# Expert stage of a small language-model tower: wide count matmuls, ups of two chunks in turn, row norm on ScalarE, top two by match and replace

## What is computed

```
h = h + attention(layernorm(h))
x = layernorm(h)                                  # rows of 128
probs, idx = top_k(softmax(x @ router_w.T), 2)    # 64 experts, two chosen
pos = place of each (token, expert) among the tokens of that expert, in order
keep = pos < 128                                  # capacity of an expert
y = gelu(x @ w1.T + b1) @ w2.T + b2               # one shared feed-forward net, 128 -> 512 -> 128
out = h + y * sum over the chosen and kept experts of their probs
```

## Time and profile before

| what | value |
|---|---|
| median of 3 runs | 1189.69 us (1189.53 to 1195.04) |
| the profiled execution's own time | 1188.89 us |
| its span, first to last instruction | 1187.0 us |
| TensorE busy | 1024.0 us (86%) |
| VectorE busy | 953.1 us (80%) |
| ScalarE busy | 756.7 us (64%) |
| GpSimd busy | 211.2 us (18%) |
| mean granted TensorE clock | 0.923 of full |

### The profile page before, as it was taken

The page is one execution under the profiler, slowest core; times in us unless marked ns, Lnnn a source line. Parts: engine busy times, 40 slices in busy tenths (PEclk is TensorE's granted clock), DMA queues, the critical chain, the costliest instruction groups (busy, mean ns, idle before and its releaser), DMA issues. The chain is left out here.

```text
span 1187.0 us, 30085 instructions
## 1 busy us (share of the span) xinstructions
PE 1024.0 (86%) x12144; PEld 545.5 (46%) x12144; DVE 953.1 (80%) x1872; ACT 756.7 (64%) x1446; POOL 211.2 (18%) x317
## 2 busy tenths in 40 slices
PE   0585777559999999999999999999999849887988
PEld 0474665403444344344443443444444225746666
DVE  3576866788998898998988988888898257979784
ACT  1557658404887878878877877787878825142332
POOL 7666845320000000000000000000000010202020
PEclk9987677857999999999999999999999987989979
DMA  3222956360332423424333342432300241314011
GB/s 76 63 77 89 200 112 209 118 133 3 56 75 38 80 51 58 72 41 71 57 60 51 58 73 38 75 56 38 73 11 12 81 150 36 93 53 124 0 35 37
DMA packets 81334, 84.06 MB, mean 71 GB/s; under 512 B 23985, under 2 KB 58358, under 8 KB 81206
## 3 DMA queue, kind: packets, MB, share of 16 engines
q1 hardware_dynamic: 70710, 73.87, 28.5%
q0 software_dynamic: 2048, 4.20, 1.5%
q10 hardware_dynamic: 8448, 4.20, 1.2%
HBM read 47.73 MB, written 34.08 MB: 69 GB/s over the span
## 5 line engine op out<-in xcount | busy, mean ns | idle before, releaser
L1114 DVE TENSOR_REDUCE b_neg_max<-psM 128x1 f32<-128x1024 f32 x512 | 603.3, 1220 | 70.1 <-PE psM L1012 66.7
L1086 ACT ACTIVATE prob<-psS 128x512 f32<-128x512 f32 x1024 | 529.1, 604 | 161.3 <-PE psS L1032 161.3
L1012 PE MATMUL psM<-ks,qs 96*32 96x512 bf16 x4096 | 418.3, 394 | 18.2 <-PEq L875 14.5
L1032 PE MATMUL psS<-qs,ks 99*32 99x512 bf16 x4096 | 407.6, 382 | 9.1 <-ACT prob L1086 4.5
L1046 PE MATMUL psO<-prob,vs 128*17 128x512 f32 x2048 | 267.2, 592 | 0.2 <-ACT prob L1086 0.2
L1032 PEld LDWEIGHTS psS<-qs,ks 99*32 99x32 bf16 x4096 | 116.0, 96 | 209.7 <-ACT prob L1086 106.9
L1012 PEld LDWEIGHTS psM<-ks,qs 96*32 96x32 bf16 x4096 | 115.6, 98 | 174.9 <-DVE b_neg_max L1114 85.9
L907 POOL CAST mpart<-b_neg_max 128x16 bf16<-128x16 f32 x32 | 6.3, 196 | 636.8 <-DVE b_neg_max L1114 624.8
L1046 PEld LDWEIGHTS psO<-prob,vs 128*17 128x17 f32 x2048 | 61.1, 99 | 50.5 <-ACT prob L1086 1.1
L329 POOL DMA_INDIRECT emb<-in_table,idx x64 | 63.3, 989 | 19.6 <-issue 14.6
L1310 ACT ACTIVATE y_t<-c_psT 128x512 f32<-128x512 f32 x16 | 9.6, 597 | 87.3 <-PE c_psT L1370 87.3
(11 more groups left out here) (134 smaller groups left out, 1058.2 us busy)
## 6 DMA issues: line engine op xcount, KB each, us to landing
qk_parts<-qk_part SPq DMA_DIRECT2D x48, 256.0 KB, 2.8
qs<-qk_parts SPq DMA_DIRECT2D x192, 64.0 KB, 3.6
ks<-qk_parts SPq DMA_DIRECT2D x96, 128.0 KB, 4.2
o_cols<-ot SPq DMA_DIRECT2D x32, 256.0 KB, 4.2
qs<-mpart_t SPq DMA_DIRECT2D x384, 1.0 KB, 1.7
v_rows<-vrow SPq DMA_DIRECT2D x16, 272.0 KB, 2.9
vs<-v_rows SPq DMA_DIRECT2D x8, 544.0 KB, 6.2
h_rows<-h SPq DMA_DIRECT2D x16, 256.0 KB, 4.9
```

What stands on the lines that cost most here:

```text
L1012: last = nc.tensor.matmul(psM[count % MRING][q * HP:(q + 1) * HP, n, :], qs[buf][0:DATA_ROWS, half, hh, at + q * HP:at + (q + 1) * HP], ks ...
L1032: last = nc.tensor.matmul(psS[unit % SRING][q * HP:(q + 1) * HP, :], ks[buf][0:ROWS, GH * gb + hh, tile * P + q * HP:tile * P + (q + 1) * HP],
L1086: nc.scalar.activation(prob[step % PRING][:, hh, :], psS[unit % SRING][:, :], ACT.Exp).then_inc(score_free, 1)
L1114: nc.vector.tensor_reduce(neg_max[e % 2][:, unit:unit + 1], psM[count % MRING][:, :, :], AX.XY, ALU.max, negate=True).then_inc(max_free, 1)
```

## The change

`count_chosen` writes the counts of all four tiles of a chunk with one matmul of 256 columns (triangle) and three of 192, 128 and 64 columns (ones), and the totals with four as before: 8 instead of 14. `up` and `gelu` go through the pieces in another order: of chunks 0 and 1 the first two pieces each, then the last two each, then chunks 2 and 3 likewise. The row norm moves from VectorE to ScalarE, as an activation with a scale and an offset for each row; GpSimd makes the offset from the negated mean, which VectorE gives it. In ScalarE's order all 16 norms of a round stand between `tanh` and `copy_y_t`; in VectorE's order `result` of chunks 2 and 3 follows `statistics`. The probabilities stay undivided by their sum, and the gate is multiplied by the inverse of the sum. `choose` finds the eight largest, overwrites all but the first two by -2, replaces the matching probabilities by -1, and marks what is below zero. The loops on the engines are written out in all five programs, so waits and addresses are constants, and `wait_apart` is used no more here. Shortened:

```diff
--- before.py
+++ after.py
...
+        PIECES = [(pair + w, k + j) for pair in range(0, WAYS, SLOTS) for k in range(0, FK, 2) for w in range(SLOTS) for j in range(2)]
+
+        def grown(r, w, k):
+
+            return r * WAYS * FK + PIECES.index((w, k)) + 1
...
-            for t in range(TILES):
-                dst = psR[w][:, 1, t * EXPERTS:(t + 1) * EXPERTS]
-                for u in range(t):
-                    nc.tensor.matmul(dst, c["ones"][:, :], chosen[w][:, u, :], start=u == 0, stop=False)
-                nc.tensor.matmul(dst, c["later"][:, :], chosen[w][:, t, :], start=t == 0, stop=True)
+            marks = chosen[w][:, :, :].rearrange("p t e -> p (t e)")
+            nc.tensor.matmul(psR[w][:, 1, :], c["later"][:, :], marks, start=True, stop=False)
+            for t in range(1, TILES):
+                nc.tensor.matmul(psR[w][:, 1, t * EXPERTS:], c["ones"][:, :], marks[:, 0:(TILES - t) * EXPERTS],
+                                 start=False, stop=t == TILES - 1)
...
                 def root(r):
                     for w in range(WAYS):
                         pool.wait_ge(eps_done, r * WAYS + w + 1)
-                        nc.gpsimd.tensor_tensor(rstd[w][:, :], var_eps[w][:, :], c["neg_half"][:, 0:TILES], ALU.pow).then_inc(rstd_done, 1)
+                        nc.gpsimd.tensor_tensor(rstd[w][:, :], var_eps[w][:, :], c["neg_half"][:, 0:TILES], ALU.pow).then_inc(root_done, 1)
+                        pool.wait_ge(root_done, r * WAYS + w + 1)
+                        nc.gpsimd.tensor_tensor(offset[w][:, :], neg_mean[w][:, :], rstd[w][:, :], ALU.mult).then_inc(rstd_done, 1)
...
-                        wait_apart(pool, h2_done, r * WAYS + w + 1 + WAYS)
+                        pool.wait_ge(h2_done, r * WAYS + w + 1 + WAYS)
...
+                def norm(r):
+                    for w in range(WAYS):
+                        act.wait_ge(rstd_done, r * WAYS + w + 1)
+                        for t in range(TILES):
+                            last = nc.scalar.activation(y[w][:, t, :], h2[w][:, t, :], ACT.Identity,
+                                                        bias=offset[w][:, t:t + 1], scale=rstd[w][:, t:t + 1])
+                        last.then_inc(y_done, 1)
...
                 def gelu(r):
-                    for w in range(WAYS):
-                        for k in range(FK):
-                            act.wait_ge(up_done, (r * WAYS + w) * FK + k + 1)
-                            src = psF[w][:, :] if k % 2 == 0 else psT[w][:, 0, :]
-                            nc.scalar.activation(hid[w][:, k, :], src, ACT.Gelu, bias=c["b1"][:, k:k + 1]).then_inc(gelu_done, 1)
+                    for w, k in PIECES:
+                        act.wait_ge(up_done, grown(r, w, k))
+                        src = psF[w][:, :] if k % 2 == 0 else psT[w][:, 0, :]
+                        nc.scalar.activation(hid[w][:, k, :], src, ACT.Gelu, bias=c["b1"][:, k:k + 1]).then_inc(gelu_done, 1)
...
                 tanh(0)
+                norm(0)
                 copy_y_t(0)
                 exponentials(0)
                 gelu(0)
-                with act.Fori(0, ITERS - 1) as it:
+                for it in range(ITERS - 1):
                     tanh(it + 1)
+                    norm(it + 1)
                     copy_y_t(it + 1)
                     exponentials(it + 1)
                     store(it)
...
                 def up(r):
-                    for w in range(WAYS):
-                        for k in range(FK):
-
-                            if k >= 2:
-                                pe.wait_ge(gelu_done, (r * WAYS + w) * FK + k - 1)
-                            elif w >= SLOTS:
-                                pe.wait_ge(gelu_done, (r * WAYS + w - SLOTS) * FK + k + 3)
-                            dst = psF[w][:, :] if k % 2 == 0 else psT[w][:, 0, :]
-                            nc.tensor.matmul(dst, c["w1"][:, k * P:(k + 1) * P], y_t[w][:, :], start=True, stop=True).then_inc(up_done, 1)
+                    for w, k in PIECES:
+
+                        if k >= 2:
+                            pe.wait_ge(gelu_done, grown(r, w, k - 2))
+                        elif w >= SLOTS:
+                            pe.wait_ge(gelu_done, grown(r, w - SLOTS, k + 2))
+                        dst = psF[w][:, :] if k % 2 == 0 else psT[w][:, 0, :]
+                        nc.tensor.matmul(dst, c["w1"][:, k * P:(k + 1) * P], y_t[w][:, :], start=True, stop=True).then_inc(up_done, 1)
...
+                        nc.vector.tensor_scalar(neg_mean[w][:, :], mv[w][:, :, 0], -1.0, None, ALU.mult)
                         nc.vector.tensor_scalar(var_eps[w][:, :], mv[w][:, :, 1], EPS, None, ALU.add).then_inc(eps_done, 1)
-
-                def norm(r):
-                    for w in range(WAYS):
-                        dve.wait_ge(rstd_done, r * WAYS + w + 1)
-                        for t in range(TILES):
-                            last = nc.vector.tensor_scalar(y[w][:, t, :], h2[w][:, t, :], mv[w][:, t, 0:1],
-                                                           rstd[w][:, t:t + 1], ALU.subtract, ALU.mult)
-                        last.then_inc(y_done, 1)
...
-                        dve.wait_ge(inv_sum_done, n)
-                        nc.vector.tensor_tensor(prob[w][:, :, :], prob[w][:, :, :],
-                                                inv_sum[w][:, :].unsqueeze(2).to_broadcast([P, TILES, EXPERTS]),
-                                                ALU.mult).then_inc(prob_done, 1)
...
                 def choose(r):
                     for w in range(WAYS):
 
-                        n = r * WAYS + w + 1
-                        wait_apart(dve, prob_done, n)
                         for t in range(TILES):
                             last = nc.vector.max(top[w][:, t, :], prob[w][:, t, :])
                         last.then_inc(top_done, 1)
                     for w in range(WAYS):
-                        n = r * WAYS + w + 1
-                        wait_apart(dve, top_done, n)
+                        dve.wait_ge(top_done, r * WAYS + w + 1)
+                        nc.vector.memset(top[w][:, :, 2:8], -2.0).then_inc(top_cut, 1)
+                    for w in range(WAYS):
+                        dve.wait_ge(top_cut, r * WAYS + w + 1)
                         for t in range(TILES):
-                            last = nc.vector.max_index(top_i[w][:, t, :], top[w][:, t, :], prob[w][:, t, :])
-                        last.then_inc(index_done, 1)
-                    for w in range(WAYS):
-                        n = r * WAYS + w + 1
-                        dve.wait_ge(index_done, n)
-                        nc.vector.tensor_copy(top_f[w][:, :, :], top_i[w][:, :, 0:2]).then_inc(index_cast, 1)
-                    for w in range(WAYS):
-
-                        n = r * WAYS + w + 1
-                        dve.wait_ge(index_cast, n)
-                        ids = c["expert_ids"][:, :].unsqueeze(1).to_broadcast([P, TILES, EXPERTS])
-                        for j, hot in enumerate((first, second)):
-                            last = nc.vector.tensor_tensor(hot[w][:, :, :], ids,
-                                                           top_f[w][:, :, j:j + 1].to_broadcast([P, TILES, EXPERTS]),
-                                                           ALU.is_equal)
-                        last.then_inc(hot_done, 1)
-                    for w in range(WAYS):
-                        dve.wait_ge(hot_done, r * WAYS + w + 1)
-                        nc.vector.tensor_tensor(chosen[w][:, :, :], first[w][:, :, :], second[w][:, :, :],
-                                                ALU.add).then_inc(chosen_done, 1)
+                            last = nc.vector.match_replace(marked[w][:, t, :], top[w][:, t, :], prob[w][:, t, :], -1.0)
+                        last.then_inc(marked_done, 1)
+                    for w in range(WAYS):
+                        dve.wait_ge(marked_done, r * WAYS + w + 1)
+                        nc.vector.tensor_scalar(chosen[w][:, :, :], marked[w][:, :, :], 0.0, None, ALU.is_lt).then_inc(chosen_done, 1)
...
+                        dve.wait_ge(inv_sum_done, n)
...
-                        nc.vector.tensor_reduce(gate[w][:, :], before[w][:, :, :], AX.X, ALU.add).then_inc(gate_done, 1)
+                        nc.vector.tensor_reduce(gate[w][:, :], before[w][:, :, :], AX.X, ALU.add).then_inc(gate_summed, 1)
+                        dve.wait_ge(gate_summed, n)
+                        nc.vector.tensor_tensor(gate[w][:, :], gate[w][:, :], inv_sum[w][:, :], ALU.mult).then_inc(gate_done, 1)
...
                 statistics(0)
-                norm(0)
                 softmax(0)
                 choose(0)
-                with dve.Fori(0, ITERS - 1) as it:
+                for it in range(ITERS - 1):
                     divide(it + 1)
                     silu(it + 1)
                     weigh(it, range(SLOTS))
@@ -1585,7 +1576,6 @@
                     weigh(it, range(SLOTS, WAYS))
```

(24 more changed lines are left out.)

## The result

The changed kernel takes 1197.53 us (median of 14 runs, 1193.08 to 1201.27), the kernel before 1190.96 in the same comparison (1185.91 to 1195.04): ratio 1.0051, 95% interval 1.0034 to 1.0068. That is 6.1 us slower, a little over the 0.5% (5.9 us) at which the prediction calls a time told from no change, with an interval that reaches to both sides of it; the forecast was +1.6. It is inside the range (1183.5 to 1199), above the likeliest case's own (1187 to 1196). The profiled execution took 1196.22 us, span 1194.4.

What follows compares the result with a forecast made beforehand. Rounds bound by VectorE after Tanh, then ScalarE and TensorE together, then TensorE alone. Three rounds +0.7, first +0.9, tail 0: +1.6 on 1188.89 gives 1190.5; the median lies 0.8 higher, 1191.3 us; range 1183.5 to 1199.

Steps and rivals of the forecast that it cites:

- +1.6: Whole kernel: net us added to the profiled execution, from +0.7 in three rounds, +0.9 in the first, tail 0.
- the likeliest case: Routing at half clock in every round, ups then with little or no wait: 1187 to 1196 us, chance 0.60.
- slower cases: Clock lost before the fifth up, 1197 to 1201 us, or no head start from the order, 1204; slower: 0.22.
- Choosing, counts, loops: VectorE's choosing under the Gelus, count matmuls during Tanh, jumps of written-out loops: each 0 us on the path.
- Gate multiply and mean: VectorE half of a round: four gate multiplies at 0.19 and a negated mean at 0.08, 0.84 us on the path.
- Row norm: ScalarE: 16 norms at 0.385 us before the first copy; transpose 3 3.46 us late, routing at half clock every round.
- The rival in which the clock stays up: Routing keeps full clock: 50.4 us a round, 9.9 less in three, 1181, or 1187 if lost later; chance 0.15.
- Output issues: ScalarE between last exponential and first Gelu: written-out loops drop register arithmetic at four issues, 0.54 us saved a round.
- Ups in turn: TensorE runs four ups before the first Gelu, then twelve of 0.86 us with little or no wait.
- The rival in which the clock is lost there: TensorE's wait before the fifth up loses the clock: 2 to 3.3 us a round, 1197 to 1201; chance 0.17.
- the third rival: Order of ups gives no head start: first up to Tanh keeps 21.0 us, +4.2 each round, 1204; chance 0.04.
- its +0.9: First round: later norms and routing at half clock put the next Tanh at 1007.3 against 1006.44, +0.9 us.

Runs made afterwards that it cites:

- e6: Kernel before with its five loops written out and nothing else: 1190.65 us, ratio 0.9986.
- e4: Changed kernel with probabilities divided by their sum again and no gate multiply, match-and-replace kept: 1191.43 us, ratio 1.0004 to the kernel before.
- e8: Changed kernel with unread matmuls added in TensorE's idle time ahead of and between the transposes: 1186.95 us, ratio 0.9947 to the kernel before.
- e3: Changed kernel with up projections and Gelus in the old order, chunk after chunk: 1208.79 us, ratio 1.0151 to the kernel before.
- e2: Changed kernel with ScalarE's copies of y_t placed between the norms: 1196.13 us, ratio 1.0038 to the kernel before.
- e1: Changed kernel with the row norm back on VectorE, without negated mean and GpSimd's offset: 1182.47 us, ratio 0.9938 to the kernel before.
- e7: Changed kernel with norm on VectorE, divided probabilities without gate multiply, and outputs issued by SyncE: 1174.79 us, ratio 0.9851 to the kernel before.
- e12: As e10, but SyncE issues a round's loads ahead of the outputs: 1161.36 us, ratio 0.9743 to the kernel before.
- e13: As e10, but outputs stay on ScalarE: 1168.33 us, ratio 0.9800 to the kernel before.
- e10: As e7, with unread matmuls ahead of and between the transposes, more in the first round: 1164.40 us, ratio 0.9779 to the kernel before.
- e11: Kernel before with loops written out, ups of two chunks in turn, and outputs issued by SyncE: 1177.86 us, ratio 0.9898.
- e5: Kernel before with loops written out and ups of two chunks in turn: 1175.06 us, ratio 0.9857.

## Why the prediction was right, and where it was off

The mechanism came as forecast, step by step. The number lies 4.5 us above the forecast, and it is the range's upper end, meant for slower cases that did not occur, that still holds it: that much is luck. Times of the third round, counted from its Tanh (1064.99; 1059.83 in the working):

| step | predicted | measured |
|---|---|---|
| first root | 20.84 | 21.31 |
| norm begins | 22.13 | 22.63 |
| first copy of y_t | 28.28 | 28.80 |
| transpose of chunk 2 | 28.92 | 29.42 |
| first up | 37.42 | 37.90 |
| last exponential | 38.59 | 39.07 |
| first Gelu | 41.99 | 42.71 |
| fifth up | 42.73 | 43.45 |
| next Tanh | 53.7 | 54.64 |

- **Choosing, counts, loops: 0.** Right. Match-and-replace takes 0.21 us and 0.08 for loading its values, about what the index search took (0.21 and 0.07), and Silu waits longer than before (5.69 us for 4.69). In e6 no stall of a jump can be told: -1.7 us, interval -4.1 to +0.8. The Trainium skill has a rule by which a taken branch can stall (Runtime: NRT & Kernel Launch, Instruction fetch mechanics); no run here shows it.
- **Gate multiply and mean: 0.84.** Mis-sized: the root comes 1.31 later than before (21.31 against 20.00), and e4 gets 1.2 back. A chunk's weighing, sum to sum, takes 2.11 us (1069.63 to 1071.74) where it took 1.83: 0.28 a gate multiply, above the 0.16 to 0.25 allowed for it.
- **Row norm.** Right: (6.26 - 0.48)/15 = 0.385 each, the routing at 1.2 GHz in all four rounds. The rival in which the clock stays up did not come true; the working gave it 9.9 us in three rounds, and e8 got 12.4 back by the ratios, 7.3 by the profiles.
- **Output issues: 0.54 saved.** Mis-sized: last exponential to first Gelu takes 3.64 us, 0.30 less than 3.94.
- **Ups in turn.** Right: four ahead of the Gelus, 0.53 us of wait, then 0.86 each, but the fifth took 1.13. The rival in which the clock is lost there did not occur: not in this wait of 0.53 us, and not in e8's of 1.90 either, where the fifth up again took 1.12. What the order is worth is what the third rival had worked out for its absence: 4.2 us a round, 12.6 in three; e3 lost 11.9.

The step that failed is the sum's size: these three small terms make 0.47 + 0.24 + 0.27 = 0.98 us, the third round's whole difference from 53.7, and all three rounds have them. Two more are stretches that the sum had at full clock. In the first round, 1.9 us over its +0.9, the projections of chunks 1 and 2 (timeline of the changed kernel; before 1.53 and 1.06) help to put the root 1.13 us later against Tanh (0.08 in the sum), and the third up was slow as well. But e6, the kernel before with its loops written out, has nearly the same projections there (1.91 and 1.49), so this loss is not shown to come from the change.

```profile
965.91 1.92 PE L1373 MATMUL c_psF<-w_o_sb,so 128*128 128x128 f32 x8
...
968.04 1.56 PE L1373 MATMUL c_psF<-w_o_sb,so 128*128 128x128 f32 x8
...
995.30 1.57 PE L1407 MATMUL c_psF<-y_t,w_sb 128*128 128x512 f32 x2
```

In the second round the projections of chunks 2 and 3 took 1.6 us longer than in the third (3.86 us from the wait's end for 2.23), at a granted clock of 0.55 and 0.58; it was 1.00 ahead of the wait:

```profile
1016.72 0.48 PE L138 MATMUL c_psF<-bias_parts,ones 65*128 65x512 bf16 x1 [1.88 <-DVE h L1468]
1016.99 1.92 PE L1373 MATMUL c_psF<-w_o_sb,so 128*128 128x128 f32 x8
1018.69 0.63 PE L138 MATMUL c_psF<-bias_parts,ones 65*128 65x512 bf16 x1
1019.12 1.62 PE L1373 MATMUL c_psF<-w_o_sb,so 128*128 128x128 f32 x8
```

The wait ahead of them is 1.88 us where the kernel before waits 1.27, since two gate multiplies now stand ahead of the residual that TensorE waits for. Without them, in e4, it is 1.30. Timelines of the kernel before, then of e4:

```profile
1013.92 0.39 PE L138 MATMUL c_psF<-bias_parts,ones 65*128 65x512 bf16 x1 [1.27 <-DVE h L1453]
1014.15 1.06 PE L1357 MATMUL c_psF<-w_o_sb,so 128*128 128x128 f32 x8
```
```profile
1023.92 0.39 PE L138 MATMUL c_psF<-bias_parts,ones 65*128 65x512 bf16 x1 [1.30 <-DVE h L1468]
```

Over all the profiles the slow pair goes with this wait. The five kernels with gate multiplies, where it is 1.88 to 2.17 us in each of the last three rounds, have the pair in one of these rounds: the second (changed, e2), the third (e3) or the last (e1, e8). Where it is 1.27 to 1.46 us (before, e4 to e7, e12, e13) no such projection was slow. In the rounds of e10 and e11 where VectorE is later still and the wait is 2.21 to 2.76 us, the second of the two was (1.68 to 1.79 us). So the term for the gate multiplies, which the working took as VectorE's time alone, most likely cost these 1.6 us too, by way of TensorE's clock; the working knew only waits of 2.6 to 3.9 us that lost it. With one profile of each kernel that is not shown, and why one round has the pair and the next, with the same wait, has not stays open.

What the sum did not show is that its +1.6 was a difference of two large parts. By the ratios: ups in turn -15.4 (e5 against e6), norm on ScalarE +13.5 (e1), gate multiply +5.6 (e4), loops -1.7 (e6), together +2.0 where +6.1 was measured. With the order's worth inside the changed kernel, 11.9 (e3), in place of 15.4 the sum is +5.5. With 3 to 4 us of uncertainty on each part, the rest cannot be placed.

## What to carry to other kernels

Undo each part of a bundled change alone: here one part was worth as much as another cost, and the total hid both. Moving work from a busy engine to a freer one was dear here because it lengthened TensorE's idle ahead of its next stage, which then ran at half clock in all four rounds; some unread matmuls in the gap, sized by round, gave that back. A transfer moved to another queue must not stand ahead of loads that are due sooner.

## What the runs showed of the hardware

- Once at 1.2 GHz, TensorE stayed there through 6.93 us of routing without a break (32 fp32 matmuls of 64 columns, mean 418 ns), and had the full clock again by the third up in that round (2.02, 1.49, then 1.02 us).
- A program can have either clock in equal stages: e1's second routing took 6.92 us, its third 1.90 and 1.97. The changed kernel's projections behind a wait of 1.88 us had half the clock in the second round and the full clock in the third.
- ScalarE's norm of a 128x128 fp32 tile steps at 0.385 us, VectorE's at 0.31: 1.2 us a round for 16. The choice of engine cost 13.5 us (e1), so more by way of TensorE's clock, for which e8 got 12.4 back with the norms still on ScalarE, than by the rate. The Trainium skill puts VectorE at up to about three times ScalarE's rate, in bf16 (ScalarE: Activation LUTs, Rules for kernel authors); in fp32 the two steps here differ by a factor of 1.25.
